# Cross-attention in a decoder layer: softmax maximum ahead of the previous batch's normalisation, row term ahead of both, context copies ahead of exp

## What is computed

```
Q = einsum('btx,dx->btd', x1, Wq) + bq
K = einsum('bpx,dx->bpd', ctx, Wk) + bk
attn = softmax(einsum('btd,bpd->btp', Q, K) / sqrt(1024))
x2 = layernorm(x1 + einsum('btp,bpd->btd', attn, ctx))
```

## Time and profile before

| what | value |
|---|---|
| median of 3 runs | 2069.47 us (2069.39 to 2072.95) |
| the profiled execution | 2066.55 us |
| its span in the trace | 2064.8 us |
| mean granted TensorE clock | 0.971 of full speed |
| PE matmul busy | 1916.6 us, 93% of the span |
| VectorE, ScalarE, GpSimd busy | 42%, 23%, 16% |

### The profile page before, as it was taken

How to read it: one execution, slowest core, us unless ns; L and a number is a source line. 1 busy time by engine, 2 the same in 40 slices (tenths; PEclk the granted TensorE clock), 3 DMA queues, 4 the chain that set the end, 5 groups by cost and what they waited for, 6 DMA issues and landing times.

```text
span 2064.8 us, 28785 instructions
## 1 busy us (share of the span) xinstructions
PE 1916.6 (93%) x11206; PEld 1108.2 (54%) x11206; DVE 864.8 (42%) x1298; ACT 474.5 (23%) x788; POOL 329.9 (16%) x263
## 2 busy tenths in 40 slices
PE   4899988898888886899999999999999999999998
PEld 2666634677777775454454444544544544444443
DVE  6677546644455554534434444344344321101111
ACT  2221001555455443222222222222222200000000
POOL 0222365111111111111111212111111000000000
PEclk9999999999999998899999999999999999999999
DMA  8342499232333331121121121121211232212220
GB/s 291 98 117 75 139 296 258 78 97 87 110 105 113 104 96 34 34 56 35 40 56 41 32 56 41 40 48 41 55 37 36 70 116 97 77 68 96 96 96 20
DMA packets 148776, 179.97 MB, mean 87 GB/s; under 512 B 102641, under 2 KB 117169, under 8 KB 146542
## 3 DMA queue, kind: packets, MB, share of 16 engines
q1 hardware_dynamic: 142222, 175.12, 29.2%
q10 hardware_dynamic: 6496, 4.06, 0.8%
HBM read 135.68 MB, written 43.46 MB: 87 GB/s over the span
## 4 chain that ended last, share of the span: by engine, by line
PE 52%; issue 33%; DVE 7%; DMA 3%; POOL 3%; ACT 2%; SPq 0%; POOLq 0%; ACTq 0%; DVEq 0%
PE psum L1295 48%; DMA arena<-in_L_xattn_Wq 2%; POOL small L939 1%; DVE arena L719 1%; PE psum L1438 1%; POOL arena L1013 1%; DMA arena<-in_x 1%; PE psum L1550 1%; PE psum L1288 1%; DVE small L384 1%; PE psum L1568 1%; DVE arena L825 0%; DVE small L409 0%; DVE arena L402 0%; DVE small L785 0%
## 5 line engine op out<-in xcount | busy, mean ns | idle before, releaser
L1295 PE MATMUL psum<-arena 128*128 128x448 f16 (+9 forms) x9432 | 1758.7, 348 | 35.7 <-DMA arena<-in_L_xattn_Wq 14.3
L1295 PEld LDWEIGHTS psum<-arena 128*128 128x128 f16 (+5 forms) x9432 | 978.4, 107 | 793.3 <-issue 113.3
L1038 POOL TENSOR_TENSOR arena<-arena 128x1024 f16<-128x1024 f32 (+1 forms) x65 | 139.1, 2140 | 685.4 <-ACT arena L1238 685.4
L879 DVE SCALAR_TENSOR_TENSOR arena<-psum,small,arena 128x448 f32<-128x448 f32 x84 | 57.4, 684 | 417.8 <-PE psum L1295 417.8
L919 DVE SCALAR_TENSOR_TENSOR arena<-psum,small,arena 128x512 f32<-128x512 f32 x28 | 21.0, 751 | 333.2 <-PE psum L1295 322.2
L939 POOL TENSOR_TENSOR small<-small 112x1 f32<-112x1 f32 (+1 forms) x46 | 38.5, 838 | 590.0 <-DVE small L389 590.0
L1238 ACT ACTIVATE arena<-arena 128x1024 f16<-128x1024 f32 (+1 forms) x65 | 68.7, 1057 | 270.3 <-DVE arena L865 270.3
L1438 PE MATMUL psum<-ident_f,arena 128*128 128x128 f16 (+1 forms) x768 | 66.6, 252 | 55.4 <-ACT arena L1138 53.8
L1251 ACT ACTIVATE arena<-arena 128x448 f16<-128x448 f32 (+1 forms) x88 | 50.7, 577 | 292.2 <-DVE arena L879 292.2
L1438 PEld LDWEIGHTS psum<-ident_f,arena 128*128 128x128 f16 (+1 forms) x768 | 54.3, 113 | 67.5 <-ACT arena L1138 59.3
L1013 POOL TENSOR_TENSOR arena<-arena 128x224 f16<-128x224 f32 x64 | 39.5, 617 | 265.4 <-ACT arena L1132 265.4
(11 more groups left out here) (188 smaller groups left out, 874.6 us busy)
## 6 DMA issues: line engine op xcount, KB each, us to landing
arena<-in_ctx SPq DMA_DIRECT2D x62, 512.0 KB, 3.8
h_scratch<-arena SPq DMA_DIRECT2D x88, 224.0 KB, 2.7
arena<-h_scratch SPq DMA_DIRECT2D x13, 1408.0 KB, 6.0
arena<-in_x SPq DMA_DIRECT2D x32, 448.0 KB, 5.4
x_scratch<-arena SPq DMA_DIRECT2D x32, 448.0 KB, 3.1
arena<-in_ctx SPq DMA_DIRECT2D x31, 448.0 KB
arena<-x_scratch SPq DMA_DIRECT2D x30, 448.0 KB, 4.5
arena<-in_L_ffn_down_qweight SPq DMA_DIRECT2D x21, 512.0 KB
```

What stands on the lines that cost most here:

```text
L879: dve.scalar_tensor_tensor(h_f[0:n, :], up[0:n, :], sc_u[0:n, :], g_act[0:n, :], ALU.mult, ALU.mult).then_inc(s_hf, 1)
L1038: pool.tensor_tensor(dst[1], src, dst[0], ALU.subtract).then_inc(s_wl, 1)
L1295: mm = pe.matmul(out, a, r, start=(k == 0), stop=(k == len(pairs) - 1))
```

## The change

On VectorE the layernorm of batch n moves out of iteration n and stands in iteration n+1 behind `softmax_in`; the last one follows the loop. The row term of n+1 moves up to stand right behind the x1 low parts. Since it now writes its `yo` slot in the iteration in which PE transposes batch n-1 out of it, it gets a wait on `s_x2t`. GpSimd's power moves with the layernorm, to the head of the next iteration. On ScalarE the copies of context transposes 0 to 3 move ahead of exp, and so ahead of g chunk 0. PE's and SyncE's programs are the same.

```
@@ row_term (VectorE)
                 dve.wait_ge(s_yout[b % 2], 16 * NB // 2 + slot_fills(n, b))
+
+                if not known(n, 2):
+                    dve.wait_ge(s_x2t, 2 * (n - 1))
                 dve.tensor_tensor_reduce(yo[0:S, b % 2, :], xr3[0:S, b % 2, :], u_b[0:S, :], 1.0, 0.0,
@@ cross_attention (VectorE)
+            def normalise(n, b):
+                y = yo[0:S, b % 2, :]
+                norm_stats(y, NB + n, s_y3, 2 * n + 1)
+                norm_apply(y, NB + n, s_n)
+
             def cross_attention(g, more):
                 for b, n, has in batches(g, more):
-                    y = yo[0:S, b % 2, :]
                     softmax_in(n, b)
+                    if not known(n, 1):
+                        normalise(n - 1, (b + 1) % 2)
                     if has(2):
                         pick_factors(n + 2, (b + 2) % GB)
...
                     if more:
                         x1t_lo(n + GB, b, 4)
+                    if has(1):
+                        row_term(n + 1, (b + 1) % GB)
                     if has(2):
                         context_lo(n + 2, (b + 2) % GB, 0)
...
                         context_lo(n + 2, (b + 2) % GB, 2)
-                    norm_stats(y, NB + n, s_y3, 2 * n + 1)
-                    if has(1):
-                        row_term(n + 1, (b + 1) % GB)
-                    norm_apply(y, NB + n, s_n)
...
             cross_attention(NG - 1, False)
+            normalise(NB - 1, (NB - 1) % 2)
@@ cross_attention (GpSimd)
+                    if not known(n, 1):
+                        inverse_std(NB + n - 1, S)
                     if has(2):
                         for k in range(4):
                             g_lo(KC + 4 * n + k, 4 * (b % 2) + k, 1 - b // 2)
-                    inverse_std(NB + n, S)
...
             cross_attention(NG - 1, False)
+            inverse_std(2 * NB - 1, S)
@@ cross_attention (ScalarE)
+                    if has(1):
+                        context_t(n + 1, CT_ACT[:4])
                     act.wait_ge(s_lm, n + 1)
                     act.activation(sp_[0:S, 0:CTX], sp_[0:S, 0:CTX], ACT.Exp, bias=nm3[0:S, :],
                                    accum_out=rs3[0:S, b:b + 1]).then_inc(s_ex3, 1)
                     if has(2):
                         g_out(KC + 4 * n, 4 * (b % 2), 1 - b // 2)
-                    if has(1):
-                        context_t(n + 1, CT_ACT[:4])
```

More of the change, by code:

```diff
@@ L769, in cross_attention @@
                         context_lo(n + 2, (b + 2) % GB, 2)
[L770 to L773, removed]
             k = [0]
```

## The result

The changed kernel is faster: 2019.6 us median of 4 runs (2013.2 to 2030.1) against 2071.2 for the kernel before (2069.4 to 2084.7), ratio 0.9745 with a 95% interval of 0.9715 to 0.9775. That is 53 us, or 47 to 59; the forecast was 54.6 us won and 2015 us. One execution was profiled, and it was the longest of the four: 2030.06 us, span 2028.3 us. It lost time ahead of the change: the first logits of cross-attention stand at 418.6 us, before at 407.0. It took 406.0 us before (406.98 to 812.95) and 357.4 us now (418.56 to 775.92). What follows it is the same within 1 us: 2064.8 - 812.9 = 1251.9 and 2028.3 - 775.9 = 1252.4.

The account below looks back on a forecast made before the run. PE bounds the kernel, losing time in cross-attention to waits and slow clock. A steady batch of 22.06 + 0.8 + 1.0 = 23.9 us saves 3.8; 49 - 1 + 5.9 + 0.7 = 54.6 won, 2015 us, range 2002 to 2033.

Parts of the forecast that it names:

- The bound and the place: Cross-attention: PE, busy 93%, loses 5.6 us a batch above its work, mainly second context transposes waiting for ScalarE's copies.
- The chain after the change: Steps from a batch's logits: maximum at 7.7 us at the latest, attended at 14.9, a new wait of 0.8 us.
- The collision: Row term and GpSimd's low part of g chunk 3 meet: even batches wait 2.0 us, 1.0 a batch on average.
- Rival A: GpSimd's low part starts before the row term or interleaves: even batches keep 0.9 us, time 2006 us; chance 0.27.
- The rule on the shared port pair: VectorE and GpSimd at SBUF: whichever starts first locks the pair; with it the forecast sum, without it 2006 us.
- The sum: Batches 1 to 13 win 49 us, batch 0 loses 1, batch 14 wins 5.9, batch 15 0.7: 54.6, giving 2015 us.
- rival B: PE's clock still falls: once per two batches (first case) 2025 us, once in each 2036; chance 0.22.
- Rival C: Nothing won: another wait, say PE's for the row term, takes each batch back to 27.7 us; 2069 us; chance 0.05.
- the 3.40 and the 1.31 are gone: Second four context transposes on PE: 3.40 us idle before them and 1.31 us of slow clock in them vanish.
- D: Slower: PE's clock stays at 1.2 GHz after attended's 0.8 us wait; 2132 us at 9 us of work; chance 0.04.

Follow-up runs that it names:

- row term last: The changed kernel with VectorE's row term of the next batch behind all context low parts instead of ahead; stage 343.8 us, median 2005.6 us, ratio 0.9690.
- row term waits: The changed kernel with an added wait: the row term starts only after GpSimd's fourth low part of g; stage 349.9 us, median 2012.1 us, ratio 0.9703.
- the shortest kernel: The changed kernel with row term behind context low parts and g chunk 1's exit behind the probabilities' high parts; medians 1994.3 and 1991.7 us, ratios 0.9625 and 0.9638.
- the two profiles: The changed kernel, nothing altered, profiled in two separate runs: stage 357.4 and 353.4 us, medians 2019.6 and 2021.4 us.
- the vector part alone: The changed kernel with ScalarE's old order, exp and g chunk 0 ahead of the copies; stage 353.1 us, median 2016.5 us, ratio 0.9721.
- copies only: The kernel before with only ScalarE's context copies 0 to 3 moved ahead of exp; stage 369.3 us, median 2030.8 us, ratio 0.9814.
- the run with g chunk 1 late: The changed kernel with ScalarE's exit of g chunk 1 moved behind the probabilities' high parts; stage 343.3 us, median 2006.8 us, ratio 0.9668.
- the run with the layernorm only: The kernel before with only the layernorm, and GpSimd's power with it, moved behind the next batch's softmax; stage 363.3 us, median 2027.7 us, ratio 0.9811.

## Why the prediction was right, point by point

**The bound and the place**: right. The wait for the copies and the half clock behind it were most of the 5.6 us by which a batch exceeded PE's work; both are gone from the steady batches.

**The chain after the change**: right in its steps. Attended starts 14.93 us after its logits (578.23 - 563.30; predicted 14.9) and waits 0.98 us (0.8). A batch with no wait for GpSimd behind it was to take 22.06 + 0.8 = 22.9; batch 6 took 22.80. That this fits so closely is partly luck, as the sum below shows. In batch 15 attended began 9.1 us after the logits (9.4). ScalarE goes from copy 3 straight to exp, and GpSimd's power takes 0.55 us, since the row term no longer runs beside it. In odd batches the maximum is out 8.05 us after the logits, where the prediction had 7.7 at the latest, and still 1.9 us ahead of ScalarE:

```profile
593.61 0.54 DVE L681 TENSOR_REDUCE small<-logits 112x1 f32<-112x375 f32 x1
596.07 0.63 ACT L1176 ACTIVATE logits<-logits,small 112x375 f32<-112x375 f32 x1
```

**The collision**: right in place and size, by a margin that the prediction called a hair: the row term starts 0.04 us first. The two runs that separate the pair (row term last, row term waits) bring the even wait from 1.9 back to 0.86. Rival A, no collision, did not occur; its price of some 8 us lies between what those two runs won in the stage, 10 to 14 us and 3.5 to 7.5.

**The rule on the shared port pair** (the Trainium skill, "SBUF — State Buffer", section "SBUF: two separate sides") says that whichever of the two engines starts first keeps the pair for its whole instruction and the other is blocked. The trace agrees in both directions: the second to come sits out most of what is left of the first, 1.65 against 0.61 us on GpSimd, 2.82 against 2.48 for two low parts on VectorE. The prediction priced only the first direction.

**The sum**: 54.6 predicted; 48.6 in the stage of the first profile and 52.6 in the second (53.9 predicted there), 53 by whole executions. The steady batch took 24.2 us instead of 23.9, and that small error is what is left of larger ones. Too much: PE's work at full clock is 21.64 us (the even batches of the shortest kernel) and not 22.06. The clock had cost more than the 1.31 us that were taken off, since the exp transposes ran slowly too (0.56 us from start to start in the earlier trace rows, 0.31 now, 574.48 to 574.79), and 2.46 for g chunk 1 was its duration, where start to start it takes 2.30. Too little: with attended's wait a batch is 1.16 us above that work, not 0.8; the clock still fell behind two of the six 1.9 us idles of batches 2 to 12, 1.67 us each (a third of the first case of rival B); and odd batches wait 0.40 us on context low parts. And batch 14 took 19.65 and 15.86 us in the two profiles, 17.6 predicted; the clock decides there.

**What the prediction had wrong.** Rival C gave the row term's place "a cover of about 4 us". The cover was none: the context low parts of n+2 are what the next first transposes wait for, and today they end at 600.83 where those transposes start at about 601.0. The working counted them to 6.1 us beside transposes at 6.18 and did not draw the conclusion. It cost 0.40 us in odd batches, 0.34 of it the lengthened low parts on VectorE, which the prediction left out, and the run with the added wait showed 0.71. The second error is of attribution: "the 3.40 and the 1.31 are gone" was put down to the copies' new place. By the runs the vector part alone removes nearly all of it, and the copies' place is worth nothing beside the early row term. So the forecast time was right for a change of which one part was not needed.

**Rivals B, C and D.** C and D did not occur; in batches 1 to 13 the clock fell twice, for 1.67 us lost each time, and never stayed low for a batch. Of B a third came. Its thought that many small idles bring the clock down was backed with a batch of 22 us from the earlier trace rows; those rows show only some 10 us at full clock behind the 0.85 us idle, up to the idle of 3.40. The run "copies only" is the better test: PE idles three to four times in each batch there, 0.3 to 1.4 us at a time, and the clock fell in none of batches 1 to 13.

## What to carry to other kernels

When a wait has two causes in a row (copies behind a softmax behind a layernorm), moving either helps, the two gains do not add, and only runs of the parts and of pairs of them tell which part pays: here one of three moves cost 10 to 14 us in the version that was made. Before moving an instruction with two SBUF inputs on VectorE, look up what GpSimd does at the new place, and do not count a gap as cover until the consumer of everything behind it has been found. After the main wait has gone, walk the chain of the engine that is late next: one exit of g moved behind what attended waits for gave another 10 to 14 us.

## What the runs showed that I had not expected

The granted clock is not settled by the length of the idle in front. With the same even wait of 1.9 us it fell behind two of the six in batches 2 to 12 in both profiles of the change and in the run with VectorE's part only, and behind four of six in the run with g chunk 1 late, where PE otherwise idles less; with waits of 0.86 us, in the four kernels that moved or held the row term of the change, it fell in no steady batch. It can fall behind less than 1.9 us: in the run with the layernorm only it fell in batches 1 and 5, behind an idle of 1.0 to 1.1 us and three of under 0.2, and not in the other odd batches, whose idles are as long or longer. Why it falls behind one 1.9 us idle and not behind the next stays open. Below, windows of 1 us in the changed kernel, about 2 us behind the start of an even batch's logits that had waited 1.92 us, and as far behind another's that had waited 1.89 (the clock is the number after the last bracket):

```profile
515.00:516.00 1.00, 1.00 (x5) 0.65 (x4) 1.00 (x2) 0.65 (x1) 0.00 (x0) 0.50 0.78 61
565.00:566.00 1.00, 1.00 (x8) 0.82 (x7) 1.00 (x3) 0.49 (x1) 0.00 (x0) 1.00 0.54 82
```

Whole executions of one kernel differ by up to 17 us while the stage repeats within 4: the rest is ahead of cross-attention. Among the twelve profiles the first logits stand between 405.8 and 418.6 us, and that goes with VectorE's wait for staged context: in the five that start at 412.6 or later it waited 57 to 61 us, in the seven that start at 410.0 or earlier 44 to 52. That the transfers are the cause was not tested.
